# Where the two transposes of hid stand in the routed part of a mixture-of-experts kernel

## The reference

```python
def _moe(x, w, sel, gate_proj, up_proj, down_proj):
    cw = (jax.nn.one_hot(sel, NUM_EXPERTS, dtype=x.dtype) * w[..., None]).sum(1)
    def body(acc, inp):
        g, u, d, we = inp
        y = jax.nn.silu(x @ g.T) * (x @ u.T) @ d.T
        return (acc + we[:, None] * y, None)
...
shared = jax.nn.silu(x @ shared_gate.T) * (x @ shared_up.T) @ shared_down.T
return (out + shared).reshape(B, S, H)
```

## Time and profile before

| What | Value |
|---|---|
| Median of 3 runs | 825.34 us (824.69 to 826.1) |
| The profiled execution's own time | 825.98 us |
| Its span | 824.2 us |
| PE busy | 811.2 us (98%) |
| DVE / ACT / POOL busy | 484.9 / 388.9 / 433.2 us |
| Granted PE clock | 0.997 of full speed |
| Chain that ended last | PE 94% of the span |

### The profile page before, as it was taken

How to read it: one execution, slowest core, us unless ns; L and a number is a source line. 1 busy time by engine, 2 the same in 40 slices (tenths; PEclk the granted TensorE clock), 3 DMA queues, 4 the chain that set the end, 5 groups by cost and what they waited for, 6 DMA issues and landing times.

```text
span 824.2 us, 19365 instructions
## 1 busy us (share of the span) xinstructions
PE 811.2 (98%) x4133; PEld 650.2 (79%) x4134; DVE 484.9 (59%) x1017; ACT 388.9 (47%) x782; POOL 433.2 (53%) x399
## 2 busy tenths in 40 slices
PE   9999999999999999999999999999999999999996
PEld 5568778888887888888888888888888878888884
DVE  5788899627444446644457446647567456464541
ACT  4864334435344345534455445546455455354432
POOL 5503111635566556566565666555654664765533
PEclk9999999999999999999999999999999999999998
DMA  8985967999999899899998999998998999999955
GB/s 291 392 332 172 252 141 217 250 218 268 229 255 236 166 198 179 202 284 234 185 192 193 281 225 189 210 286 173 244 262 183 273 237 217 235 196 174 191 70 73
DMA packets 145305, 181.52 MB, mean 220 GB/s; under 512 B 30570, under 2 KB 103922, under 8 KB 142834
## 3 DMA queue, kind: packets, MB, share of 16 engines
q0 software_dynamic: 37776, 89.08, 52.5%
q1 hardware_dynamic: 106528, 80.45, 37.6%
q10 hardware_dynamic: 834, 10.49, 3.6%
HBM read 82.52 MB, written 67.17 MB: 182 GB/s over the span
## 4 chain that ended last, share of the span: by engine, by line
PE 94%; DVE 2%; DMA 1%; issue 1%; ACT 0%; POOLq 0%; POOL 0%; DVEq 0%; ACTq 0%; SPq 0%
PE psGU L1112 47%; PE psY L1112 24%; PE psY L1170 5%; PE psH L983 4%; PE psGU L1153 3%; PE psGU L1154 3%; PE psGU L1155 3%; PE psT L983 1%; DMA x_ring<-x_pairs 1%; PE psY L1032 1%; PE psGU L1032 1%; PE psH L1009 1%; PE psM L1140 1%; PE psM L969 0%; DVE top L1605 0%
## 5 line engine op out<-in xcount | busy, mean ns | idle before, releaser
L1112 PE MATMUL psGU<-split_w,xT_pair 128*128 x1716 | 414.6, 390 | 0.2 <-issue 0.2
L1112 PEld LDWEIGHTS psGU<-split_w,xT_pair 128*128 128x128 f32 x1716 | 321.9, 188 | 69.5 <-issue 0.7
L695 POOL DMA_INDIRECT out<-y_ring,idx_all x143 | 226.8, 1586 | 206.1 <-SPq L584 186.8
L1759 DVE SCALAR_TENSOR_TENSOR aT<-aT,w_ring,psGU 128x256 f32<-128x256 f32 x143 | 68.6, 479 | 237.0 <-ACT aT L935 144.6
L690 POOL DMA_INDIRECT tok_ring<-h_rows,idx_all x143 | 151.3, 1058 | 70.3 <-issue 42.3
L1112 PE MATMUL psY<-split_w,hidT_hi 128*128 x564 | 187.6, 413 | 0.4 <-issue 0.4
L935 ACT ACTIVATE aT<-psGU 128x256 f32<-128x256 f32 x143 | 55.0, 385 | 253.1 <-PE psGU L1112 188.7
L841 ACT ACTIVATE y_ring<-psY 128x512 f32<-128x512 f32 x173 | 103.6, 599 | 99.2 <-PE psY L1112 45.0
L1112 PE MATMUL psY<-split_w,hidT_lo 128*128 x282 | 111.2, 394 | 0.0
L1112 PEld LDWEIGHTS psY<-split_w,hidT_hi 128*128 128x128 f32 x564 | 95.4, 189 | 13.6 <-issue 0.8
L1744 DVE STREAM_TRANSPOSE psT<-x_ring 128x512 f32<-128x512 f32 x143 | 102.4, 716 | 3.6 <-DMA w_ring<-tok_ring 3.6
(11 more groups left out here) (268 smaller groups left out, 652.3 us busy)
## 6 DMA issues: line engine op xcount, KB each, us to landing
x_ring<-tok_ring SPq DMA_DIRECT2D x284, 128.0 KB
raw_w<-ffn_w SPq DMA_DIRECT2D x17, 1536.0 KB, 9.8
out<-y_ring POOLq DMA_DIRECT2D x32, 256.0 KB
x_ring<-x_pairs SPq DMA_DIRECT2D x12, 512.0 KB, 8.4
h_rows<-tok_ring SPq DMA_DIRECT2D x16, 256.0 KB, 9.7
h_rows<-y_ring SPq DMA_DIRECT2D x16, 256.0 KB, 10.4
tok_ring<-h_rows,idx_all POOLq DMA_INDIRECT x143
out<-y_ring,idx_all POOLq DMA_INDIRECT x143
```

Of the source, the lines that this page charges most:

```text
L695: pool.indirect_dma_start(out[:, :], bass.IndirectOffsetOnAxis(idx_all[:, r:r + 1], 0), y_ring[:, r % YRING, :], None, compute_op=ALU.add) ...
L1112: mm = pe.matmul(dst, a[:, slot, c], w(at + col + k * H), start=(k == 0 and a is high and at == 0), stop=(k == parts - 1 and a is low))
L1759: v.scalar_tensor_tensor(out=hid[:, half, :], in0=gate, scalar=w_ring[:, w_slot, bass.ds(expert, 1)], in1=up, op0=ALU.mult, op1=ALU.mult). ...
```

## The change

The two transposes of hid of tile t-1 are issued in the middle of the first layer of tile t, between its parts k=1 and k=2, and no longer behind it; `down(t-2)` follows the first layer directly. `split_product` has a new argument `between`, a table from part number to a function that is called ahead of that part. Steps of routed tile 0 and of the last tile keep their order. `xpose_hid` now always waits for `hidT_ready`. The waits themselves, the data and the other engines' code are the same.

```diff
-            def xpose_hid(t, n):
+            def xpose_first(t):
                 pe.wait_ge(hid_ready, t.done(1))
-                if n is None or n >= 1:
-                    pe.wait_ge(hidT_ready, t.done())
-                transposes(psH, hid[:, t.slot % 2, :], IK).then_inc(hid_xposed, 1)
+                pe.wait_ge(hidT_ready, t.done())
+                pe.transpose(psH[:, 0:P], hid[:, t.slot % 2, 0:P], ident[:])
+
+            def xpose_second(t):
+                pe.transpose(psH[:, P:2 * P], hid[:, t.slot % 2, P:2 * P], ident[:]).then_inc(hid_xposed, 1)
+
+            def xpose_hid(t):
+                xpose_first(t)
+                xpose_second(t)
...
-            def split_product(dst, high, low, slot, parts, w, col):
+            def split_product(dst, high, low, slot, parts, w, col, between):
 
                 for k in range(parts):
+                    if k in between:
+                        between[k]()
                     c = slice(k * P, (k + 1) * P)
...
-                gate_up(t, n, kept[-1], needed)
                 if n == NT:
+                    gate_up(t, n, kept[-1], needed, {})
                     for k in range(GROUP):
                         shared_down(NT // GROUP - 1, k)
-                else:
-                    xpose_hid(t + -1, None if n is None else n - 1)
+                    return
+                gate_up(t, n, kept[-1], needed, {2: lambda: xpose_hid(t + -1)})
                 if n is None or n >= NT + 2:
                     down(t + -2, None if n is None else n - 2,
-                         kept[-3] if j >= 2 else weights(t + -2, None if n is None else n - 2)[0])
+                         kept[-3] if j >= 2 else weights(t + -2, None if n is None else n - 2)[0], {})
```

More of the change, by code:

```diff
@@ L1114, in split_product, with gate_up @@
                 return mm
-            def gate_up(t, n, w, needed):
+            def gate_up(t, n, w, needed, between):
                 if needed is not None:
@@ L1123, in gate_up, with down @@
                     pe.wait_ge(hid_ready, t.done(-1))
-                split_product(psGU[t.slot % 2][:], xT_hi, xT_lo, t.slot % 2, HK, w, 0).then_inc(gu_done, 1)
-            def down(t, n, w):
+                split_product(psGU[t.slot % 2][:], xT_hi, xT_lo, t.slot % 2, HK, w, 0, between).then_inc(gu_done, 1)
+            def down(t, n, w, between):
                 pe.wait_ge(hidT_ready, t.done(1))
@@ L1129, in down @@
                     pe.wait_ge(y_ready, t.done(-1))
-                split_product(psY[t.slot % 2][:], hidT_hi, hidT_lo, t.slot % 2, IK, w, UP).then_inc(down_done, 1)
+                split_product(psY[t.slot % 2][:], hidT_hi, hidT_lo, t.slot % 2, IK, w, UP, between).then_inc(down_done, 1)
             def fill_slots(g):
@@ L1221, in step @@
                 if n == LAST:
-                    down(t + -2, n - 2, weights(t + -2, n - 2)[0])
-                    xpose_hid(t + -1, n - 1)
-                    gate_up(t, n, kept[-1], needed)
+                    down(t + -2, n - 2, weights(t + -2, n - 2)[0], {})
+                    xpose_hid(t + -1)
+                    gate_up(t, n, kept[-1], needed, {})
                     return
-                gate_up(t, n, kept[-1], needed)
                 if n == NT:
+                    gate_up(t, n, kept[-1], needed, {})
                     for k in range(GROUP):
                         shared_down(NT // GROUP - 1, k)
-                else:
-                    xpose_hid(t + -1, None if n is None else n - 1)
+                    return
+                gate_up(t, n, kept[-1], needed, {2: lambda: xpose_hid(t + -1)})
                 if n is None or n >= NT + 2:
                     down(t + -2, None if n is None else n - 2,
-                         kept[-3] if j >= 2 else weights(t + -2, None if n is None else n - 2)[0])
+                         kept[-3] if j >= 2 else weights(t + -2, None if n is None else n - 2)[0], {})
             def xpose_last_hid():
```

## The result

The changed kernel took 832.13 us in the median of 4 executions (830.28 to 836.78), the kernel before 825.02 us beside it (824.07 to 826.1). The ratio is 1.0088, with a 95% interval of 1.0047 to 1.0128. Run once more it was 831.71 us, ratio 1.0095 (1.0072 to 1.0119). So it is slower by about 7 us; forecast were 829.0 us, a range of 825.2 to 832.6, and slower with a chance of 0.74.

A forecast was written before the change was run, and what follows sets the result against it. PE was taken to bound the kernel, busy in 98% of the span. Losses of 0.43 + 0.85 + 0.74 + 0.79 + 0.89 = 3.70 us on the profiled 825.98 gave 829.7, a median of 829.0 us, range 825.2 to 832.6.

The forecast's parts named there:

- The deadline: Time from the transposes' old place to the end of `split_hid` before PE waits: 2.58 us, before the change 4.18.
- Ordinary tiles: Routed tiles with `split_hid` ending after 1.62 us, 0.96 us under the limit: no cost.
- rival B: Faster: a pair of transposes inside one accumulation costs less than 0.235 us; 822.0 us at 0.05 a tile; chance 0.09.
- rival C: Much slower: PE's own issue falls behind after a late release, 0.1 us in each of 140 tiles, 843 us; chance 0.10.
- The bound of +3.5 us: Upper end if a pair between two halves of a first layer costs 0.025 us more over some 140 tiles.
- The start: Between the first layers of tiles 1 and 2, with no second layer as cover: loss 0.43 us, once.
- The loop entry: Where DVE enters its loop, idle 5.05 us before the mix: loss 1.77 us, net 0.85 us.
- Behind the loop: Two tiles after DVE's loop, DVE idle 4.01 us: loss 0.74 us, before nothing.
- Tiles that prepare weights: DVE's 1.2 us weight piece stands ahead of the mix; five tiles over the limit: together 0.79 us.
- Tile 110: DVE's transposition of x waits for a late transfer: loss 2.85 us, 1.96 already lost, net 0.89; possibly -1.96.
- A: No change: the cover suffices, late tiles are fewer in another execution and tile 110 isn't late; 825.9 us, chance 0.17.
- D: Slower: each of six back edges of DVE's loop stalls as its entry does, up to 1.77 us, 839.6 us; chance 0.06.

The follow-up runs named there:

- the four distances: Changed kernel with the pair of transposes ahead of first-layer part 3, 2 (the change itself), 1 or 0: 827.7, 832.1 and 831.7, 843.4, 898.4 us.
- half change: Changed kernel with the new transpose place only in PE's loop (96 tiles); the 47 straight-code tiles keep the old order: 827.61 us, ratio 1.0024.
- shifted loop: Changed kernel with DVE entering its loop four tiles earlier, at tile 12, and leaving it at tile 140: 835.49 us, ratio 1.0117.
- the order behind the second layer: Changed kernel with the transposes of t-1 moved behind the second layer of t-2 instead of inside the first layer: 829.11 us, ratio 1.006.
- the later mix: One more DVE operation ahead of every mix: added to the kernel before 826.2 us, ratio 0.9999; to the changed kernel 834.88 us, ratio 1.012.

## Why the prediction was right, and where it was off

**The deadline.** The prediction's limit of 2.58 us, from 1.365 + 1.365 us of cover less 0.15, held: the pair stands 2.75 us behind the beginning of the second layer, follows a late `split_hid` by 0.14 us, and the four distances gave times in the order of their limits, with 4.74 to 4.79 us measured for 4.75 in the one case where every tile waits.

**Ordinary tiles cost nothing.** Right, and so rival B (a cheaper pair) and rival C (PE's own issue falls behind) are out for the ordinary tile: the period stayed at 4.33 to 4.35 us, and with the pair ahead of part 0, where the release comes last of all, it was 4.74 to 4.79. The bound of +3.5 us for a pair inside an accumulation wasn't needed.

**The start**, forecast 0.43 us: from the second transposition of the one pair to that of the next are 3.43 us (199.06 - 195.63), in the kernel before 3.00. Right.

**The loop entry**, forecast a loss of 1.77 us ahead of the pair: the gap was 1.72 us. Right in this execution, 0.95 to 2.49 in the others.

**Behind the loop**, forecast 0.74 us: the gap was 1.87 us, and the three tiles there took 15.02 us and not 13.06, so 1.96 us more. This term was mis-sized. It was read from DVE's idle time of 4.01 us in one execution, and in the changed kernel that was 5.28. That both idle times of DVE "stay as long" was the step that failed: over the five traces of the changed kernel they were 4.5 to 6.0 us at the entry and 4.0 to 5.9 us behind the loop. Cover is what made this variation free before, and it was cut.

**Tiles that prepare weights**, forecast 0.79 us together, at five tiles. In the profiled execution of the change, the gaps of this kind were at other tiles: for one, tile 72 had L of 510.53 - 507.47 = 3.06 us and a gap of 0.30, while tile 30 had none. From the first layer of tile 18 to that of tile 109 the changed kernel took 396.58 us and the kernel before 394.79, so 1.79 us more: this term was mis-sized too. The half change puts all that lies in the loop at 1.4 to 2 us. The advance of 0.235 us by the earlier second layer was right (0.46 to 0.23).

**Tile 110**, forecast +0.89 us: the transfer wasn't late in the changed kernel's profile, so neither the 1.96 us of before nor the 2.85 came, and the five tiles from 109 on took 22.90 us in place of 23.68. That was the lower bound that the prediction gave for it. The event isn't unique, though. DVE waited for that transfer in five of the 14 traces: 3.60 us in the kernel before, 2.15 us in the changed kernel's execution of 837.87 us, 2.78 in the half change, 2.48 with the pair ahead of part 3 and 1.24 with the shifted loop. The forecast of a median should have had it with its share and not whole.

**The sum.** 3.70 us were forecast over the profiled execution, 4.3 came there, and about 7 in the medians. That 3.70 and 4.3 are near is in part luck: by stretches of the two traces 0.47 us came for 0.43 at the start, 1.18 for 0.85 at the loop entry, 1.96 for 0.74 behind the loop, 1.79 for 0.79 in the tiles between, and -0.78 for +0.89 at tile 110, so terms that were too small and one of the wrong sign cancel in good part (the rest, -0.3 us, lies elsewhere). It is in part luck too that 832.13 lies in the range: its upper end of 832.6 was set in view of 3.5 us for a dearer pair, which cost nothing, and two of the four executions, 833.5 and 836.78 us, lie above it. What lies between 4.3 and 7 is the spread: the changed kernel's executions reach from 830 to 838 us. The prediction took each event's length from the one trace as if fixed. Longer events cost the changed kernel in full, and the prediction had no term for the clock, which in three of five traces of the changed kernel fell to the lower level behind a gap. The kernel before has a spread of its own, 822.45 to 833.21 us, of which the sum, made from one execution, knows nothing. The prediction's terms also had DVE and the transfer as the only late parties; it had none for ACT's silu.

**Rivals A and D.** A (the cover suffices everywhere) is out: it holds for the ordinary tile, but the gaps are there in all five traces. D (a stall at each turn of DVE's loop) is out as it was put: only entry and exit have one that comes back. The 1.77 us at each of six back edges didn't come. At tiles 48, 64 and 80 the idle time ahead of the mix in the first profile is 2.48, 2.39 and 2.37 us, where ordinary tiles have 2.1 to 2.3, and at 32 and 96 it is 1.01 and 0.99, as in the kernel before (1.01 and 1.00). At the sixth, tile 112, it is 2.01 us and not 1.21, and PE lost 1.00 us there, in two other of the five traces 0.54 and 0.60. With the 4.00 us at tile 60 of the shifted loop that leaves room for a stall at a back edge now and then. The rule of the Trainium skill that the prediction weighed puts a stall at taken branches, and these rows hardly bear that out. That the trace agrees with it at the entry said more than the row gives, which is idle time with no releaser.

Open are the cause of DVE's long idle times at the entry of its loop and behind it, why that at the entry was gone with the shifted loop, why the stretch ahead of tile 0 grew in that kernel, and why ACT's silu is now and then 2 to 4 us late.

## What to carry to other kernels

When an operation is moved towards its producer on the engine that bounds the kernel, subtract the cover that is left (what that engine does between) from the lateness of the producer in every tile, not in the ordinary one: the ordinary tile had 1 us to spare here, and the gaps were in four to nine tiles of 143. Read how late the producer can be from more than one execution, and of every engine that stands ahead of it, since cover that is cut turns a harmless variation into time. And before moving it the other way, count the consumer's cover too, as the order behind the second layer showed.

## What the runs showed of the hardware that was not expected

- A gap of PE of 2.0 to 3.2 us in a stretch that is otherwise fully busy was in seven cases followed by some 3.5 us at, or mostly at, the lower clock of 1.2 GHz, with 0.43 us a matmul and not 0.23. In the changed kernel the gaps were 2.49, 2.35, 2.19 and 2.51 us, with the pair ahead of part 1 3.16, with the later mix 2.00 (granted 0.51 from 268.5 to 272 us), and with the pair behind the second layer 1.99 (0.61 from 768 to 771.5 us). Other gaps of about the same length weren't followed by one: 2.49 us at 767.64 in the execution of 831.55 us, the 1.99 us behind the loop in that of 837.87, and 1.92 us at the entry in the half change. A matmul that takes 0.43 us in place of 0.23 puts out about half the work, so a whole such stretch costs some 1.6 us on top of its gap (3.5 x (1 - 0.23 / 0.43)), as the period of 5.94 us in place of 4.34 has it.
- DVE's idle time at the entry of its loop was 3.84 to 6.54 us over eleven traces of kernels in which only PE's order differed; in an ordinary tile of the changed kernel it is 2.1 to 2.3 us. Behind the loop it was 3.58 to 5.91 us in eight of them and not to be seen in the three others (the pair ahead of part 3 or part 0, and the half change).
- ACT's silu started 1.7 to 3.7 us after the end of its first layer in seven tiles of the last three traces of the changed kernel, and 2.2 to 2.9 us in five tiles with the pair behind the second layer, with no cause in the rows; an ordinary tile has 0.04 us. In the kernel before the longest was 0.7 us.
